# A smaller ring for GpSimd's DMA descriptors, and the last wait moved from GpSimd to SyncE

## The chip, the core and the metric

The kernel runs on one core of one Trainium2 chip. The metric is the time of one execution on the device in microseconds (us), the median of several runs. A core has five engines that run side by side, each with an instruction queue of its own: TensorE (PE, its weight loads as PEld), VectorE (DVE), ScalarE (ACT), GpSimd (POOL) and SyncE (SP). They are ordered among each other by semaphores alone. DMAs are issued by SP, ACT and POOL; those of POOL (here all gathers, scatters and accumulating writes) are prepared by software on GpSimd, which writes their descriptors to a scratch area in on-chip memory (SBUF).

## What is computed

The reference is one layer of a gated vision-language block on 8 sequences of 256 tokens of width 256, cut here to its core:

```python
x = x + jnp.tanh(g_xattn[0]) * _L0_xattn_ref(_layernorm(x), ctx_1024, w_q, w_kv, w_out, b_out)
x = x + jnp.tanh(g_ffn[0]) * _L0_ffn_ref(_layernorm(x), W1, W2, Wr)

# _L0_xattn_ref: 16 heads of 64, keys and values from 120 context rows
attn = softmax(einsum('bnhd,bmhd->bhnm', q, k) * 64 ** -0.5)
out = einsum('bhnm,bmhd->bnhd', attn, v).reshape(b, n, 1024) @ w_out + b_out

# _L0_ffn_ref: a router chooses 2 of 8 experts for each token
topk_vals, topk_idx = jax.lax.top_k(softmax(x @ Wr.T), 2)
h = silu(einsum('btd,efd->btef', x, W1))
y = einsum('btef,edf->bted', h, W2)
out = einsum('bte,bted->btd', gate, y)
```

## The kernel before

**Tiling.** The 2,048 tokens pass through attention in 8 batches of 256. Each batch's result (x2) is stored to the output tensor, its normalized form to a scratch tensor in DRAM, and four scatters (POOL, L611, 32 in all) write its tokens' places into a table sorted by expert. Matrices are split into a high and a low half in float16, so that a product is three matmuls.

**Expert tiles.** Each token is sent to two experts, which makes 39 tiles of 128 rows, each of one expert. For tile t POOL gathers the rows (xg, L678, `gather`), PE transposes them (max_pair, L1896), multiplies by the expert's first matrix (st_bank, L1642, 48 matmuls) and second (o_bank, L1642, 24 matmuls), DVE scales the result (yt, L1489), and POOL adds it to the rows of the output tensor with an accumulating indirect DMA (out, L689, `add`). Two adds may meet the same row, so each add first waits until the one before it has landed (semaphore `y_added`, 16 counts for each). SP loads the first matrix of each tile's expert (w_tile, 1 MB, L454). Four buffers each hold xg, yt and w_tile.

**Order.** Every engine's order is written out by hand. Tiles 0 to 9 are mixed into the attention of the later batches; tiles 10 to 38 run in a loop on PE, DVE and ACT, and unrolled on POOL and SP. In this last stretch POOL's queue is, for each t, `gather(t + 4)` and then `add(t)`; the last four adds have no gather ahead. Two DMAs on POOL's queue (found, L664) read the finished table.

**The end.** POOL's last instruction before the engines meet is a wait for all 39 adds, SP's a wait for the last stores of x2.
Of the kernel before, what the change touches and what calls it, by code (L numbers as in the profile page):

```python
# [35 lines left out]
TILES = TOPK * T // P + E - 1  # L36
# [131 lines left out]
def build(nc, x, ctxT, wq, wkv, wo, bo, gx, gf, w1, w2, wr, out, xn2_dram, table, w1_dram):  # L168
    ctx = ExitStack()
    with ctx:  # L170
        def sem(name):
            return ctx.enter_context(nc.semaphore(name))
# [198 lines left out]
        y_added = sem("y_added")  # L371
# [26 lines left out]
        def _(sp):  # L398
# [118 lines left out]
                load_tile(B - 1, t)  # L517
            sp.wait_ge(x2_out[0], 16 * B)
            sp.wait_ge(x2_out[1], 16 * (B + 1))

        @block.gpsimd
        def _(pool):
# [158 lines left out]
            def add(t):  # L681
                rows = EARLY_B * N if t < EARLY else T + P
                pool.wait_ge(y_done, t + 1)
                if t in (0, EARLY):
                    for i in range(NT):
                        pool.wait_ge(x2_out[i], 16 * ((B if t else EARLY_B) + i))
                if t:
                    pool.wait_ge(y_added, 16 * t)  # L688
                pool.indirect_dma_start(out=out[0:rows], out_offset=bass.IndirectOffsetOnAxis(row_of[:, t:t + 1], 0),  # L689
                                        in_=yt[t % XG][:], in_offset=None, compute_op=ALU.add).then_inc(y_added, 16)  # L690
# [58 lines left out]
            for t in range(LISTED - 1, TILES):  # L749
                if t + XG < TILES:  # L750
                    gather(t + XG)
                add(t)
            pool.wait_ge(y_added, 16 * TILES)

        @block.scalar
        def _(act):
# [1333 lines left out]
```

## Time and profile before

| what | value |
|---|---|
| median of 3 runs | 564.67 us (564.46 to 567.79) |
| span of the profiled execution, first to last instruction | 560.1 us |
| PE busy | 493.7 us, 88% of the span |
| DVE, ACT, POOL busy | 370.2, 371.3, 363.9 us |
| DMAs of GpSimd's queue (q0) | 10.30 MB, 9.5% of the 16 engines' time |
| DMAs of SyncE's queue (q1) | 81.86 MB, 46.7% |

The span counts from the first instruction to the last. The page gives no whole time for the profiled execution; its span is 4.6 us under the median of the runs, and I take that difference as what lies around the span. "Busy" leaves out sequencer instructions such as branches, semaphores and drains, which only a query by source line shows.

### The profile page before, as it was taken

What the parts mean: (1) busy time and instruction counts of PE and PEld (TensorE: products, weight loads), DVE (VectorE), ACT (ScalarE), POOL (GpSimd) and SP (SyncE); (2) the same over time, 40 slices, a digit from 0 to 9 for tenths busy, and PEclk for the clock granted to TensorE, in tenths of its full rate; (3) what the DMA queues carried; (4) which work ended last, traced back from release to release, by engine and by line L of the source; (5) the groups of instructions that cost most, each with busy time, mean ns of one, the idle gap of its engine ahead of it and who ended that gap; (6) DMA issues with size and microseconds to landing.
All of it is one profiled execution on the core that took longest, in us unless ns stands there. A gap on an engine that the chain in (4) does not pass through costs nothing. (4 is left out here: it accounts for less than half of the span.)

```text
span 560.1 us, 17891 instructions
## 1 busy us (share of the span) xinstructions
PE 493.7 (88%) x6630; PEld 438.3 (78%) x6631; DVE 370.2 (66%) x856; ACT 371.3 (66%) x576; POOL 363.9 (65%) x372
## 2 busy tenths in 40 slices
PE   2869799998999999798788997699999999999990
PEld 2757688887888879687567886689898898988980
DVE  5899999898889899699996664343444444343430
ACT  1838999998999899789546674245455464645530
POOL 5466979798989998788978642533544436344531
PEclk9979889999999999999689998799999999999996
DMA  7922506173553625263438598766787877778421
GB/s 286 392 77 84 175 12 219 48 244 59 175 127 119 178 97 168 33 212 73 130 148 201 153 287 145 208 185 186 214 259 201 259 207 232 229 224 244 112 30 17
DMA packets 34846, 93.13 MB, mean 166 GB/s; under 512 B 4967, under 2 KB 24565, under 8 KB 27490
## 3 DMA queue, kind: packets, MB, share of 16 engines
q1 hardware_dynamic: 25634, 81.86, 46.7%
q0 software_dynamic: 8576, 10.30, 9.5%
q8 instruction: 40, 0.66, 0.6%
q10 hardware_dynamic: 576, 0.14, 0.1%
q14 instruction: 20, 0.16, 0.1%
HBM read 74.17 MB, written 18.12 MB: 165 GB/s over the span
## 5 line engine op out<-in xcount | busy, mean ns | idle before, releaser
L689 POOL DMA_INDIRECT out<-yt,row_of x39 | 65.0, 1667 | 115.3 <-DMA out<-yt,row_of 96.5
L1642 PE MATMUL st_bank<-xsT,w_tile 128*128 128x128 f16 x1872 | 114.4, 221 | 4.3 <-issue 3.3
L1480 DVE SCALAR_TENSOR_TENSOR hT<-hf,h_scale,hT 128x512 f16<-128x512 f32 x78 | 58.6, 754 | 88.1 <-ACT hT L974 88.1
L1642 PEld LDWEIGHTS st_bank<-xsT,w_tile 128*128 128x128 f16 x1872 | 109.2, 99 | 7.0 <-issue 5.4
L1642 PE MATMUL o_bank<-w2s,hT 128*128 x936 | 109.9, 274 | 1.2 <-DVE yt L1489 1.1
L1642 PEld LDWEIGHTS o_bank<-w2s,hT 128*128 128x128 f16 x936 | 90.4, 99 | 12.4 <-issue 1.6
L968 ACT ACTIVATE hf<-st_bank,z_scale 128x512 f32<-128x512 f32 x78 | 52.9, 679 | 47.9 <-PE st_bank L1642 40.4
L592 POOL TENSOR_TENSOR pT<-pT 120x512 f16<-120x512 f32 x64 | 77.3, 1221 | 8.0 <-ACT pT L842 7.7
L974 ACT ACTIVATE hT<-hf,h_scale 128x512 f16<-128x512 f32 x78 | 56.3, 722 | 13.1 <-ACT hf L968 4.5
L637 POOL TENSOR_SCALAR stage<-stage,upw 128x512 f32<-128x512 f32 x32 | 55.9, 1748 | 10.5 <-ACT w_hi L941 10.4
L841 ACT ACTIVATE pT<-st_bank,exp_bias,logit_scale 120x512 f32<-120x512 f32 x64 | 50.0, 781 | 12.1 <-PE st_bank L1858 11.6
L842 ACT ACTIVATE pT<-st_bank,exp_bias,logit_scale 120x512 f16<-120x512 f32 x64 | 50.1, 783 | 0.0
L949 ACT ACTIVATE xsT<-max_pair 128x256 f16<-128x256 f32 x39 | 14.9, 382 | 48.8 <-PE max_pair L1896 44.7
L678 POOL DMA_INDIRECT xg<-xn,row_of x39 | 39.8, 1019 | 11.3 <-issue 8.9
L1778 PE MATMUL j_bank<-wos,oT 128*128 128x256 f16 x384 | 45.4, 272 | 0.3 <-DVE oT L1179 0.3
L1642 PE MATMUL o_bank<-v,pT 120*128 120x65 f16 x768 | 35.1, 197 | 11.7 <-DVE o L1367 9.6
L1642 PEld LDWEIGHTS o_bank<-v,pT 120*128 120x128 f16 x768 | 30.3, 99 | 18.2 <-issue 16.2
L611 POOL DMA_INDIRECT table<-entry,slot x32 | 32.9, 1027 | 14.2 <-DVE entry L1324 7.2
L1642 PE MATMUL j_bank<-xnT,wqs 128*128 128x256 f16 x336 | 41.0, 273 | 0.3 <-DVE oT L1179 0.3
L1778 PEld LDWEIGHTS j_bank<-wos,oT 128*128 128x128 f16 x384 | 36.4, 98 | 4.5 <-DVE oT L1179 0.4
L1344 DVE TENSOR_REDUCE max_pair<-max_pair 128x8 f32<-128x960 f32 x32 | 37.0, 1155 | 0.0
L1489 DVE TENSOR_SCALAR yt<-o_bank,gate_y 128x256 f32<-128x256 f32 x39 | 18.9, 483 | 25.4 <-PE o_bank L1642 25.2
(217 smaller groups left out, 966.5 us busy)
## 6 DMA issues: line engine op xcount, KB each, us to landing
w_tile<-w_split SPq DMA_DIRECT2D x39, 1024.0 KB, 5.2
stage<-in_w SPq DMA_DIRECT2D x16, 1024.0 KB, 5.1
w_split<-w_hi SPq DMA_DIRECT2D x8, 512.0 KB, 2.8
w_split<-stage SPq DMA_DIRECT2D x8, 512.0 KB, 3.9
out<-x SPq DMA_DIRECT2D x17, 128.0 KB, 5.4
xin<-in_x SPq DMA_DIRECT2D x8, 256.0 KB, 4.7
w2s<-in_wkv SPq DMA_DIRECT2D x2, 1024.0 KB, 12.2
xres<-in_x SPq DMA_DIRECT2D x16, 128.0 KB
```

Of the source, the lines that this page charges most:

```text
L592: pool.tensor_tensor(pT[g % 2][:, 1, h, :], pT32[:, h, :], pT[g % 2][:, 0, h, :], ALU.subtract).then_inc(pT_low[h], 1)
L637: chain.link(pool.tensor_scalar(chunk, chunk, upw[q % 2][:, i:i + 1], None, ALU.mult))
L678: pool.indirect_dma_start(out=xg[t % XG][:], out_offset=None, in_=xn2_dram[0:rows], in_offset=bass.IndirectOffsetOnAxis(row_of[:, t:t + 1] ...
L689: pool.indirect_dma_start(out=out[0:rows], out_offset=bass.IndirectOffsetOnAxis(row_of[:, t:t + 1], 0), in_=yt[t % XG][:], in_offset=None, ...
L841: nc.scalar.activation(pT32[:, h, :], st_bank[h][0:M, :], ACT.Exp, bias=exp_bias[0:M], scale=logit_scale[0:M])
L842: nc.scalar.activation(pT[g % 2][:, 0, h, :], st_bank[h][0:M, :], ACT.Exp, bias=exp_bias[0:M], scale=logit_scale[0:M]).then_inc(exp_done[h ...
L968: nc.scalar.activation(hf[par][:, cols], z_bank[a][:], ACT.Silu, scale=z_scale[:, bass.ds(t, 1)]).then_inc(silu_done, 1)
L974: nc.scalar.activation(hT[par][:, 0, 4 * a:4 * a + 4, :], hf[par][:, cols].rearrange("p (c n) -> p c n", c=4), ACT.Copy, scale=h_scale[:, ...
L1344: ins = nc.vector.tensor_reduce(both[:, t].rearrange("p (h c) -> p h c", h=2), max_pair[:, :, 0:HP * M].rearrange("p h (c m) -> p h c m", ...
L1480: nc.vector.scalar_tensor_tensor(out=hT[par][:, 1, 4 * a:4 * a + 4, :], in0=hf[par][:, 512 * a:512 * a + 512].rearrange("p (c n) -> p c n" ...
L1642: ins = pe.matmul(out, lhs[i](a), rhs[i](c), start=(i == 0 and a + c == 0), stop=(i == n - 1 and a == 1))
L1778: ins = pe.matmul(dst[:, 0:D], oT[t][:, a, ic, :], wos[:, c, ic, :], start=(ic + a + c == 0), stop=(ic == IC - 1 and a == 1))
```

## The change

```diff
@@ -517,6 +517,7 @@
                 load_tile(B - 1, t)
             sp.wait_ge(x2_out[0], 16 * B)
             sp.wait_ge(x2_out[1], 16 * (B + 1))
+            sp.wait_ge(y_added, 16 * TILES)
 
         @block.gpsimd
         def _(pool):
@@ -750,7 +751,6 @@
                 if t + XG < TILES:
                     gather(t + XG)
                 add(t)
-            pool.wait_ge(y_added, 16 * TILES)
 
         @block.scalar
         def _(act):
@@ -2076,7 +2076,7 @@
...
-    nc = bacc.Bacc("TRN2", target_bir_lowering=False, num_devices=1)
+    nc = bacc.Bacc("TRN2", target_bir_lowering=False, num_devices=1, dynamic_dma_scratch_size=8192)
```

The end of POOL's queue before, as the built program has it (xg is the buffer of gathered rows, yt the scaled result; x5 stands for five adds in a row, the fifth from last with tile 34):

```order
L678 DMA xg<-xn,row_of 128x256 [waits xs_full]
L689 DMA out<-yt,row_of 2176x256 [waits y_added,y_done]
L678 DMA xg<-xn,row_of 128x256 [waits xs_full]
L689 DMA out<-yt,row_of 2176x256 [waits y_added,y_done] x5
L170 UNCONDITIONAL_BRANCH [waits y_added]
```

and now:

```order
L679 DMA xg<-xn,row_of 128x256 [waits xs_full]
L690 DMA out<-yt,row_of 2176x256 [waits y_added,y_done]
L679 DMA xg<-xn,row_of 128x256 [waits xs_full]
L690 DMA out<-yt,row_of 2176x256 [waits y_added,y_done] x5
L170 UNCONDITIONAL_BRANCH
```

POOL's branch to the end has lost its wait; the lines of POOL's code are one higher. The end of SP's queue, as the difference between the two programs:

```order
 L454 ISA
 L454 DMA w_tile<-w_split 128x4096
-L170 UNCONDITIONAL_BRANCH [waits x2_out1,x2_out0]
+L170 UNCONDITIONAL_BRANCH [waits y_added,x2_out1,x2_out0]
```

SP's branch has gained it, and nothing but the branch and SP's drain stands behind it.

## Rows read from the trace of the kernel before

**Rows 1.** Busy time by stretch: start:end, length, PE, PEld, DVE, ACT, POOL, clock, DMA.
```profile
450.00:500.00 50.00, 48.80 (x653) 45.72 (x651) 21.39 (x36) 26.55 (x44) 24.60 (x18) 1.00 0.77 231
500.00:549.00 49.00, 44.73 (x573) 41.15 (x570) 18.94 (x31) 23.26 (x37) 20.78 (x15) 1.00 0.51 129
...
552.00:556.00 4.00, 0.00 (x0) 0.00 (x0) 0.00 (x0) 0.00 (x0) 0.00 (x0) 0.50 0.00 0
556.00:560.10 4.10, 0.00 (x0) 0.00 (x0) 0.00 (x0) 0.00 (x0) 0.00 (x0) 0.50 0.00 0
```

**Rows 2.** Line L170, the end of the program: ns min/median/max, first and last start us.
```profile
L170 SPq COMPARE_BRANCH  x1: 41/41/41, 519.1 to 519.1; - x1
L170 SPq DRAIN  x1: 7/7/7, 519.3 to 519.3; - x1
L170 ACTq DRAIN  x1: 734/734/734, 541.0 to 541.0; - x1
...
L170 DVEq DRAIN  x1: 524/524/524, 546.3 to 546.3; - x1
L170 POOLq COMPARE_BRANCH  x1: 41/41/41, 551.9 to 551.9; - x1
L170 POOLq DRAIN  x1: 7780/7780/7780, 552.1 to 552.1; - x1
```

**Rows 3.** Line L2079, the start of the program, POOL's drain.
```profile
L2079 POOLq DRAIN  x1: 173/173/173, 0.4 to 0.4; - x1
```

**Rows 4.** Instructions of POOL in order of time: start us, us, [idle before, releaser].
```profile
539.19 1.54 POOL L689 DMA_INDIRECT out<-yt,row_of  x1 [2.99 <-DMA out<-yt,row_of]
543.74 1.54 POOL L689 DMA_INDIRECT out<-yt,row_of  x1 [3.01 <-DVE yt L1489]
548.11 1.54 POOL L689 DMA_INDIRECT out<-yt,row_of  x1 [2.83 <-DMA out<-yt,row_of]
```

**Rows 5.** Groups of the page, POOL's DMAs: busy, mean ns, idle before.
```profile
L689 POOL DMA_INDIRECT out<-yt,row_of x39 | 65.0, 1667 | 115.3 <-DMA out<-yt,row_of 96.5
...
L678 POOL DMA_INDIRECT xg<-xn,row_of x39 | 39.8, 1019 | 11.3 <-issue 8.9
...
L611 POOL DMA_INDIRECT table<-entry,slot x32 | 32.9, 1027 | 14.2 <-DVE entry L1324 7.2
```

**Rows 6.** Instructions that touch the table's read-back (found).
```profile
L664 POOL DMA_INDIRECT found<-table,blk x2: 917/977/1037, 273.4 to 360.4; - x2
```

**Rows 7.** DMA queues, 545 to 561 us (two adds): packets, MB, share.
```profile
q0 software_dynamic: 288, 0.26, 14.5%
```

**Rows 8.** Chain of waits, 476 to 491 us: start us, us, what.
```profile
479.13 0.71 issue
479.84 4.19 DMA out<-yt,row_of
...
484.08 1.18 issue
485.25 4.46 DMA out<-yt,row_of
...
489.76 0.71 issue
```

**Rows 9.** POOL's groups from 381.7 us to the end.
```profile
L689 POOL DMA_INDIRECT out<-yt,row_of x30 | 50.0, 1668 | 83.7 <-DMA out<-yt,row_of 78.3 <-DVE yt L1489 3.0 <-issue 2.4
L678 POOL DMA_INDIRECT xg<-xn,row_of x26 | 26.5, 1021 | 7.9 <-issue 5.5 <-PE max_pair L1896 2.4
```

**Rows 10.** Instructions of POOL, 379 to 389 us, in order of time.
```profile
379.92 1.55 POOL L689 DMA_INDIRECT out<-yt,row_of  x1 [4.09 <-DMA out<-yt,row_of]
381.77 1.44 POOL L678 DMA_INDIRECT xg<-xn,row_of  x1 [0.30 <-issue]
388.36 1.57 POOL L689 DMA_INDIRECT out<-yt,row_of  x1 [5.16 <-DMA out<-yt,row_of]
```

**Rows 11.** The PE row that uses the rows gathered at 381.77.
```profile
387.83 0.44 PE L1896 MATMUL max_pair<-ident,xg 128*128 128x128 f32 x2
```

**Rows 12.** Gathers from 370 us on: issue to landing.
```profile
DMA to landing us min/median/max: 2.7/3.3/4.9
```

**Rows 13.** Adds from 360 us on: issue to landing.
```profile
DMA to landing us min/median/max: 3.6/4.8/7.7
```

## The prediction

> **What bounds the kernel now.** I read the busy time by stretch first. From 450 to 500 us PE works 48.80 of 50 us [rows 1]: the expert loop is bound by PE, a tile (48 + 24 + 2 matmuls) taking 50 / (653 / 74) = 5.7 us. The chain of waits names the DMA of the adds for almost all of this stretch, but that is a chain that runs beside PE: an add lands a median 4.8 us after its issue [rows 13], and with the 0.71 us from landing to next issue [rows 8] makes a cycle of 5.5 us, just under PE's 5.7. The change removes nothing from this stretch.
>
> The same view shows what the change aims at: from 552 us to the end at 560.1 us no engine computes and no DMA moves a byte [rows 1]. The page's list of groups cannot say what fills these 8.1 us, as it leaves sequencer instructions out. The query of the end's line does [rows 2]: POOL's branch, held back by its wait for the last add, executes at 551.9 us, and then POOL's DRAIN takes 7,780 ns, from 552.1 to 559.9 us. ACT's drain takes 734 ns and DVE's 524, behind compute of their own. SP's, with 39 tile loads and all the stores and loads of the kernel on its queue before it, takes 7 ns. POOL's first drain, before it has issued a DMA, takes 173 ns [rows 3]. So a drain is not slow for the DMAs' bytes, nor on POOL as such: it is slow on POOL after POOL's DMAs. There are 39 adds, 39 gathers, 32 scatters and 2 reads of the table [rows 5, 6], 112 in all, so 7,780 / 112 = 69 ns for each, if the drain visits every one. That it does so is my inference from these rows.
>
> **What is around it.** The last add is issued at 548.11 us and POOL is done with it at 549.65 [rows 4]; it lands where the branch is released, at 551.9 [rows 2]. From the drain's end to the end of the span are 560.11 - 559.88 = 0.23 us, in which POOL collects and releases the others. The profiled execution stands for the runs: its span is 4.6 us under their median of 564.67, and I keep these 4.6 us.
>
> The Trainium skill, VectorE: DVE Perf Modes, section "The DRAIN you can't avoid", calls the drains of the preamble and postamble "~12 ns constant" on all five engines. By that rule there would be nothing to gain here. The trace agrees for SP (7 ns [rows 2]) and disagrees for POOL by 7,768 ns, and the measurement decides that the time exists; what is left of the rule is a rival below.
>
> **Part 1: the wait goes from POOL to SP.** POOL's branch no longer waits. It follows the last add's issue at 549.65, and the drain starts 0.2 us later, as in rows 2: 549.85 instead of 552.1, so 2.25 us earlier. Behind the wait on SP there is only SP's branch and its 7 ns drain; no load or store queues behind it, and SP has been idle since 519 us [rows 2]. SP sees the landing at 551.9, its branch and drain take 0.2 us, and POOL needs that signal to release the end. So the span cannot end before 552.1 + 0.23 = 552.35 us, which is 7.76 us under 560.11. With the drain as long as now it would end at 549.85 + 7.78 + 0.23 = 557.86, 2.25 us under.
>
> **Part 2: half the scratch.** If the drain visits DMAs that nobody has retired yet, the scratch bounds their number: what has to be overwritten has to be retired first. Each add puts 288 / 2 / 16 = 9 packets on each DMA engine [rows 7], and 112 x 9 = 1,008 for the whole kernel. No row shows how many the scratch holds. Between the ends "as long as now" (7.78 us) and "as short as at the start" (0.17 us [rows 3]), half a scratch that is full at the end means at most half the 112: 56 x 69 ns = 3.9 us, end 549.85 + 3.9 + 0.23 = 553.98, 6.1 us under.
>
 No run yet shows it.
>
> A drain of up to (552.1 - 549.85) / 0.069 = 32 DMAs would be hidden behind the landing. A ring that frees only a part of its entries at a time fills up once more before the end and leaves fewer than 56; one that frees all 56 at the 57th leaves 56 again. The saving is therefore 6.1 to 7.8 us. I take 7.5, because a retirement late in the program is likely with either number of descriptors and anything under 32 entries is worth the full 7.76.
>
> **Part 3: retiring in line.** What the drain no longer does, POOL must do while issuing. Two rows bound it. Above: 3.9 us at once, 56 at the drain's 69 ns. Below: once in the kernel before the step from landing to issue is 1.18 us where it is 0.71 elsewhere [rows 8], 0.47 us more, at the 92nd of POOL's DMAs; that may be one retirement of this kind, since a ring would need it about there if an add took more descriptors than a gather. I take 0.47 us, because a retirement in line needs one look at an old semaphore and not 56.
> Where does it fall? From 381.7 us on there are 30 adds and 26 gathers [rows 9], so the gather at 381.77 us is the 57th DMA, and the first to overwrite if 56 fit. POOL idles 5.16 us behind it [rows 10], so the add chain does not feel it; PE wants those rows at 387.83 [rows 11], and the landing is at most 381.77 + 4.9 = 386.7 [rows 12], 1.1 us early. 0.47 us is hidden; 3.9 us would cost up to 2.8 us. Later retirements on an add lengthen its cycle, which has 0.2 us to PE's 5.7 and four buffers behind it: hidden, unless it is one of the last adds. There the add at 543.74 was released by DVE and the one at 548.11 by the add before [rows 4]; one retirement of 0.47 us between costs 0.1 to 0.3 us.
>
> **The sum.** Outside the tail nothing; tail -7.5; in line +0.2: -7.3, so 564.67 - 7.3 = 557.4 us, a span of 552.8. The cover of part 1 is the last add's flight; were the drain shorter still, the landing at 551.9 is what is late next. Everything in SBUF moves down by 8192 bytes; I cost that at nothing, since all tiles move together and no engine's instruction changes.
>
> The Trainium skill, Runtime: NRT & Kernel Launch, section "The ~15µs preamble/postamble breakdown", puts about 2 us behind a kernel for resetting the DMA rings. If half the ring halved that, the result would be 1 us lower, an estimate from that page, and inside the range; no row shows the time around the span.
>
> **The rivals.**
> - *The drain's length does not depend on the scratch* (it visits all 112, or a fixed area). For: nothing in the trace varies the scratch. Against: nothing. It starts 2.25 us earlier all the same: 562.4 us. Chance 0.12.
> - *The drain is fixed work that starts once the last DMA has landed.* Then the move hides nothing: 564.6 us. The rule of the constant drain belongs here: nothing moves. Against it stand 173 ns at the start and 7,780 at the end. Chance 0.06.
> - *Retiring costs as much in line and meets PE.* The 57th DMA takes 3.9 us more or waits for the add ahead of it; PE stalls 1 to 2.8 us, or several late adds each lose a part of it. 564.67 - 6.1 or 7.5, + 1 to 2.8: 558.2 to 561.4 us. Chance 0.17.
> - *Slower: every DMA behind the 56th waits until the one before it has landed,* as the ring is always full from there. Then a gather waits for the add ahead of it, and the cycle is 4.8 (landing) + 0.7 + 1.0 (gather) + 0.3 = 6.8 us, 1.1 over PE's 5.7 for each of 26 gathers: +29 us, and -6 at the end: 588 us. It decides from the point where the cycle passes 5.7 us. Against: a full ring frees its oldest entry, which landed long ago. Chance 0.03.
>
> **Numbers.** The forecast has 0.62, with a range of its own of 556.6 to 558.8 us. A measurement here tells 1%, 5.65 us, from no change: faster means 559.0 or less. That is the forecast and about 0.04 of the third rival: 0.66. Within 1%: 0.31. Slower: 0.03. The range has to reach from the forecast over the third rival to the first, which leaves 0.09 out: 556.0 (the floor of 556.9 less 0.9 for scatter of the runs, and the ring's reset) to 562.6 us.
>
> **What would show it.** Right: POOL's drain starts within 0.3 us of 549.9 (or the last add's end) and takes under 3.9 us; SP's branch follows the last landing; the span ends 0.4 us behind it. A gather near the 57th DMA, or the step before an add, is longer by some tenths. Wrong: the drain still takes 7.8 us (first rival), starts behind the landing (second), PE waits for xg near 388 us (third), or gathers start only where adds land (fourth).

## The result and the profile after

The changed kernel took 553.78 us in the median of 5 runs (552.65 to 556.34), against 564.67 us before (564.38 to 567.79, 5 runs): ratio 0.9839, 95% interval 0.9801 to 0.9876. (All ratios and intervals here and below leave out executions over 1.5% above the fastest of their kernel, so they are nearer to 1 than the medians, which are of all.) It is faster, as forecast. The forecast of 557.4 us was 3.6 us too high, and the range (556.0 to 562.6) missed the time.

The profiled execution of after has a span of 553.3 us, 6.8 us less than before. The query of the end's line, which answers to [rows 2], shows what went (columns: instructions, ns min/median/max, first and last start us):

```profile
L170 ACTq DRAIN  x1: 732/732/732, 541.4 to 541.4; - x1
...
L170 DVEq DRAIN  x1: 524/524/524, 546.7 to 546.7; - x1
L170 POOLq DRAIN  x1: 4543/4543/4543, 548.5 to 548.5; - x1
L170 SPq COMPARE_BRANCH  x1: 41/41/41, 552.6 to 552.6; - x1
L170 SPq DRAIN  x1: 7/7/7, 552.8 to 552.8; - x1
```

POOL's drain no longer begins behind the landing of the last add. Its record begins at 548.5 us, even before that add's own record, which ends at 550.26; counted from there it takes 548.50 + 4.54 - 550.26 = 2.78 us where before it took 7.78. SP's branch now shows the landing (552.6), where POOL's did.

The page's instruction groups of POOL, which answer to [rows 5], are as they were:

```profile
L690 POOL DMA_INDIRECT out<-yt,row_of x39 | 64.2, 1645 | 115.6 <-DMA out<-yt,row_of 101.9
...
L679 POOL DMA_INDIRECT xg<-xn,row_of x39 | 39.6, 1015 | 11.3 <-issue 9.2
...
L612 POOL DMA_INDIRECT table<-entry,slot x32 | 32.5, 1014 | 15.1 <-DVE entry L1324 8.0
```

So are the stretches of the loop, which answer to [rows 1] (columns as there); the third line is the empty time at the end, of which 0.7 us is left from 8.1:

```profile
450.00:500.00 50.00, 48.74 (x649) 45.64 (x647) 21.66 (x36) 26.49 (x44) 25.04 (x18) 1.00 0.76 229
500.00:549.00 49.00, 45.14 (x580) 41.55 (x577) 18.98 (x31) 23.64 (x38) 19.75 (x15) 1.00 0.52 131
...
552.60:553.20 0.60, 0.00 (x0) 0.00 (x0) 0.00 (x0) 0.00 (x0) 0.00 (x0) 0.50 0.00 0
```

I call **tail** the time from the end of DVE's last yt (tile 38) to the end of the span, and **loop** the time from tile 13's yt to tile 37's. In after the tail is 553.28 - 547.18 = 6.10 us, before 560.11 - 546.77 = 13.34: 7.24 us less. The loop took 136.86 and 136.76 us. The other 0.4 us, by which after is behind, arose before tile 13 (0.3 us: 406.75 against 406.44) and in the loop (0.1).

The chain of waits of after (start us, us, what) shows the one place where the smaller ring is seen at the end, the step of 1.35 us that is 0.71 elsewhere (its add is the 108th of POOL's DMAs):

```profile
525.41 3.88 DMA out<-yt,row_of
...
529.33 1.35 issue
530.68 3.78 DMA out<-yt,row_of
...
534.50 0.71 issue
535.22 3.84 DMA out<-yt,row_of
...
548.01 0.49 issue
548.50 1.76 POOLq L170
```

### The profile page after: what moved, and what is told of

The parts are those of the page before. It is cut to its first block and busy times, and to the rows that moved or that the text cites. A ratio compares the mean times of both kernels' runs of the same rounds, so it can differ in the third digit from the quotient of the medians.

```text
span 553.3 us, 17890 instructions
## 1 busy us (share of the span) xinstructions
PE 494.4 (89%) x6630; PEld 439.5 (79%) x6631; DVE 370.6 (67%) x856; ACT 371.4 (67%) x576; POOL 362.7 (66%) x372
## 5 line engine op out<-in xcount | busy, mean ns | idle before, releaser
L1778 PE MATMUL j_bank<-wos,oT 128*128 128x256 f16 x384 | 46.6, 277 | 0.3 <-DVE oT L1179 0.3
L1642 PE MATMUL j_bank<-xnT,wqs 128*128 128x256 f16 x336 | 42.2, 278 | 0.0
L1642 PEld LDWEIGHTS j_bank<-xnT,wqs 128*128 128x128 f16 x336 | 32.4, 99 | 4.7 <-issue 0.8
```

Of the source, the lines that this page charges most:

```text
L1642: ins = pe.matmul(out, lhs[i](a), rhs[i](c), start=(i == 0 and a + c == 0), stop=(i == n - 1 and a == 1))
L1778: ins = pe.matmul(dst[:, 0:D], oT[t][:, a, ic, :], wos[:, c, ic, :], start=(ic + a + c == 0), stop=(ic == IC - 1 and a == 1))
```

## The experiments

Theory A: the change is worth its tail, some 7.2 us, to which both edits add, and the rest of the 10.9 us between the two medians is scatter of the executions. Rival: something that the profile's span doesn't show, around the span or in the body, gives 3 us more. The others ask what the drain's length hangs on, and what retiring in line costs.

This table is worked out from the trace of each profiled execution (us). "Behind the add" is the time from the end of the last add's record on POOL to the drain's end; "Landing to end" is the time from the last landing of the last add, which releases the branch that waits for it, to the end of the span.

| kernel | scratch | wait on | drain | behind the add | last yt | tail | landing to end |
|---|---|---|---|---|---|---|---|
| before | 16384 | POOL | 7.78 | | 546.77 | 13.34 | 8.21 |
| after | 8192 | SP | 4.54 | 2.78 | 547.18 | 6.10 | 0.73 |
| e1_ring_only | 8192 | POOL | 1.70 | | 549.08 | 7.45 | 2.13 |
| e2_wait_only | 16384 | SP | 9.55 | 7.79 | 545.82 | 10.83 | 5.81 |
| e3_early_drain | 16384 | POOL | 5.52 | | 553.01 | 11.42 | 5.96 |
| e4_after | 8192 | SP | 4.39 | 2.62 | 542.81 | 6.04 | 0.73 |
| e5_ring12k_pool | 12288 | POOL | 3.66 | | 558.49 | 10.54 | 4.1 |
| e6_ring4k_pool | 4096 | POOL | 1.29 | | 542.27 | 6.78 | 1.7 |
| e7_ring6k_sp | 6144 | SP | 4.91 | 3.15 | 548.92 | 6.23 | 1.3 |
| e8_after_again | 8192 | SP | 4.47 | 2.70 | 551.04 | 5.94 | 0.73 |
| e9_late_drain | 16384 | POOL | 0.46 | | 551.82 | 11.91 | 0.9 |

**Either part alone, and both again.** e1_ring_only is before with the last line of the diff alone:

```diff
-    nc = bacc.Bacc("TRN2", target_bir_lowering=False, num_devices=1)
+    nc = bacc.Bacc("TRN2", target_bir_lowering=False, num_devices=1, dynamic_dma_scratch_size=8192)
```

> The wait stays on POOL, the scratch is 8192. Theory A (the drain and what follows the span both grow with the DMAs that are not yet retired): POOL's drain starts 0.2 us behind the last landing, as before, but takes 0.5 to 2.8 us (at most (552.56 - 550.26 + 0.48) / 0.069 = 40 DMAs, from the drain after the change) instead of 7.78, so the span is 5.0 to 7.3 us shorter than 560.1; the time around the span falls to 2 to 3 us, as with the whole change: in all 8 to 11 us faster, 554 to 557 us. Theory B (the drain is fixed work, the change gained by starting it early; what surrounds the span depends on where the last wait stands): drain 7.8 us, no gain, 564 to 565 us.

Its rows of line L170:

```profile
L170 POOLq COMPARE_BRANCH  x1: 41/41/41, 554.4 to 554.4; - x1
L170 POOLq DRAIN  x1: 1696/1696/1696, 554.6 to 554.6; - x1
```

The drain, behind the landing as before, is 1.70 us instead of 7.78: the scratch alone sets this, and the rival of a drain that visits all 112 whatever the scratch is gone. Median 557.93 us (549.78 to 561.84, 10 runs) against 564.19 (556.99 to 572.52, 31 runs) on the same chip; ratio 0.9914, 0.9842 to 0.9986. The tail is 5.9 us shorter, the medians are 6.3 apart; the expected 554 to 557 us were missed by 0.9.

e2_wait_only is before with the other two lines:

```diff
             sp.wait_ge(x2_out[1], 16 * (B + 1))
+            sp.wait_ge(y_added, 16 * TILES)
...
-            pool.wait_ge(y_added, 16 * TILES)
```

> The scratch keeps its default, the wait stands on SP. Theory A: the drain starts about 3.5 us earlier, beside the last add (after the change it stood at 548.5 where the last landing was 552.56), still retires 112 DMAs from the add's end at 549.65 on, 7.8 us, and ends near 557.5: span 557.8, 2.3 us shorter; the time around the span stays as before, so 562.4 us. Theory B (position, not size): the whole gain of 10.9 us, 553 to 555 us. Theory C (the drain's work begins at the last landing): no gain, 564.5 us.

Its rows of line L170:

```profile
L170 POOLq DRAIN  x1: 9551/9551/9551, 546.9 to 546.9; - x1
L170 SPq COMPARE_BRANCH  x1: 41/41/41, 550.9 to 550.9; - x1
```

From the last add's end (548.62) the drain takes 7.79 us, its old length, now beside the flight of 2.2 us: the tail is 2.5 us shorter. So the drain is not work that starts only at the landing, and the second rival is gone too. 561.65 us (555.08 to 571.35, 10 runs), ratio 0.9969, 0.9913 to 1.0025, which is not told from no change. The parts save 5.89 and 2.51 us of tail, together 8.4; both at once save 7.24, since with the short drain only part of it is there to be hidden.

e4_after is the changed kernel, on that chip:

> The changed kernel again, as a measure for the others on this chip: 553 to 556 us, POOL's drain 4.5 us from about 548.5, some 3 us around the span.

It took 556.63 us (550.93 to 560.68, 10 runs), 7.6 under before's median and 0.6 above the expected range; ratio 0.9936, 0.9874 to 0.9998. Its tail is 6.04 us. e8_after_again is the same, on another chip in 5 rounds:

> The changed kernel against the kernel before, five rounds. Theory A (the change acts in the tail alone, 7.2 us between the two profiles' tails of 13.34 and 6.10; the 10.9 us of the first comparison hold 3.7 us of scatter of the executions): 6.5 to 8 us faster, ratio 0.986 to 0.988. Theory B (the change also shortens the rest by 3 to 4 us, through the lower places in SBUF or fewer live descriptors): 10 to 12 us faster, ratio 0.979 to 0.982.

555.95 us (553.26 to 559.05, 6 runs) against 564.01 (556.71 to 567.87, 11 runs): 8.1 us, ratio 0.9887, 0.982 to 0.9954; tail 5.94. By their medians both repetitions lie by the tail's 7.2 us and not by 10.9. Their intervals, 0.1 to 7.1 and 2.6 to 10.2 us, end below 10.9 too, though like the ratios they lie nearer to no change than the medians do; the first ends just under the tail's 7.2 as well.

**Where the executions differ.** The profiled executions of e4 and e8 are of one program and have spans of 548.9 and 557.0 us, with tails 0.1 us apart. Their chains of waits (start us, us, what) part in the flights of the adds, e4_after:

```profile
356.23 4.01 DMA out<-yt,row_of
...
361.03 3.81 DMA out<-yt,row_of
...
366.10 4.26 DMA out<-yt,row_of
...
371.12 4.27 DMA out<-yt,row_of
```

and the same four adds in e8_after_again:

```profile
358.68 5.89 DMA out<-yt,row_of
...
365.37 5.01 DMA out<-yt,row_of
...
370.42 1.22 issue
371.64 5.62 DMA out<-yt,row_of
...
378.01 6.44 DMA out<-yt,row_of
```

They sum to 16.4 us in one and 23.0 in the other; e8 was already 2.5 us behind where the first of them is issued. Each add waits for the last, and gathers stand behind adds on POOL's queue, so PE waits for its rows in e8 (start us, us, then the instruction, and the idle time before it in brackets):

```profile
390.39 0.69 PE L1896 MATMUL max_pair<-ident,xg 128*128 128x128 f32 x2 [4.43 <-DMA xg<-xn,row_of]
```

Busy time from 385 to 405 us (columns as in [rows 1]), e4_after:

```profile
385.00:405.00 20.00, 19.26 (x263) 17.92 (x261) 7.45 (x13) 10.70 (x18) 9.78 (x8) 1.00 0.76 232
```

and e8_after_again:

```profile
385.00:405.00 20.00, 14.73 (x171) 13.41 (x170) 6.13 (x10) 6.68 (x12) 10.22 (x8) 0.91 0.66 190
```

PE, busy all through the same stretch in e4 at a granted 1.00 (2.4 GHz), stands still for 4.4 us in e8 and goes on at a mean of 0.91, part of it at the lower level of 1.2 GHz. By tile 13 e8 is 410.57 - 402.42 = 8.2 us late, and stays so to the end. In the eleven profiled executions tile 13's yt ends between 401.93 and 418.05 us, while the loop behind it takes 136.76 to 136.94 in all of them. So in the profiled executions the scatter lies ahead of tile 13 and is larger than the change. It is not the ring's doing: with the default scratch the 31 times of before spread over 15.5 us, and e5, whose first longer step comes only at its 72nd DMA, shows such a late wait of PE for xg too, 4.9 us at 397.8 (e3 as well, 4.6 us at 392.4, though its extra drain stands ahead of it). Why the same adds fly 4 us once and 6 another time I did not find.

**What sets the drain's length.** e3_early_drain and e9_late_drain keep the default scratch and the wait on POOL, and drain once more on the way, behind POOL's 45th DMA (ahead of tile 3's add) and ahead of the last five adds:

```diff
                 if b == B - 1:
+                    if t == 3:
+                        pool.drain()
                     add(t)
```

> Default scratch, wait on POOL, as before; one more POOL drain ahead of the fourth add (tile 3), where POOL idles 12.2 us for VectorE. 45 of the 112 DMAs have been issued by then. Theory A (a drain's length is the number of DMAs not yet retired, 69 ns each): the early drain takes about 3.1 us behind the landing of the third add and is hidden, the last drain takes (112 - 45) x 69 ns = 4.7 us, the span is 3.1 us shorter; if what surrounds the span grows with the same number, another part of 4 x 45/112 = 1.6 us: 560.0 to 561.5 us. Theory B (the scratch's size sets the drain, whatever is in it): last drain 7.8 us, 564.5 us.

```diff
                 if t + XG < TILES:
                     gather(t + XG)
+                if t == TILES - 5:
+                    pool.drain()
                 add(t)
```

> Default scratch, wait on POOL, one more POOL drain behind the last gather and ahead of the fifth-last add (tile 34), where no idle time covers it. Theory A (retiring is work that moves): that drain takes about 107/112 x 7.78 = 7.4 us behind the landing of the last gather, the last drain 0.3 to 0.7 us (5 DMAs), the last five adds come some 6 us later and catch up little; tail from VectorE's last result to the end 12 to 13.5 us, about as before. Theory B (only the drain at the end is slow, whatever is left to retire): two drains of 7.8 us, tail 19 us or more.

The drains of e3, by their lines (the extra one is L699):

```profile
L699 POOLq DRAIN  x1: 12488/12488/12488, 339.6 to 339.6; - x1
...
L170 POOLq DRAIN  x1: 5523/5523/5523, 558.7 to 558.7; - x1
```

and of e9 (the extra one is L753), with POOL's DMAs around it in order of time:

```profile
L753 POOLq DRAIN  x1: 9979/9979/9979, 530.3 to 530.3; - x1
...
L170 POOLq DRAIN  x1: 460/460/460, 563.0 to 563.0; - x1
```

```profile
531.90 1.00 POOL L678 DMA_INDIRECT xg<-xn,row_of  x1 [0.30 <-issue]
541.07 1.56 POOL L689 DMA_INDIRECT out<-yt,row_of  x1 [8.16 <-issue]
545.88 1.67 POOL L689 DMA_INDIRECT out<-yt,row_of  x1 [3.25 <-DMA out<-yt,row_of]
```

The last drain is shorter by what has been drained before: 5.52 us for the 67 DMAs since, 0.46 us for 5. So the length is in the DMAs not yet retired, which was the inference of part 2, and nothing in the scratch as such. Less the 173 ns of an empty drain [rows 3] it is 57 ns for each of 5, 80 for each of 67, and 68 for each of 112 if none of those was retired before.

e3's tail is 1.9 us shorter, and its median (562.38 us, 558.49 to 566.92, 10 runs) is 1.8 lower (560.0 to 561.5 were expected); its ratio of 1.0004 (0.9954 to 1.0053) is not told from no change. The extra drain was expected to take 3.1 us behind the landing. POOL's DMAs around it:

```profile
339.97 1.59 POOL L689 DMA_INDIRECT out<-yt,row_of  x1 [0.30 <-issue]
352.89 1.57 POOL L689 DMA_INDIRECT out<-yt,row_of  x1 [11.33 <-issue]
```

It can work from 341.56 us, where the 45th DMA is issued, and 45 DMAs at 80 ns each would be done by 345.3. It ends at 352.09. The 45th, an add, lands 10.2 us after its issue, at 350.2: the drain ends 1.9 us behind that and delays the next add by as much. So it seems to have waited for the DMA in flight, and an extra drain cannot simply be put anywhere. e9's, from the gather's end at 532.90 to 540.3, takes 7.4 us and moves the work ahead of five adds that come one by one; the last add starts 7.4 us behind the last yt, and 1.4 us of the tail are won (11.91; one execution, 566.79 us).

**Retiring in line.** e5_ring12k_pool and e6_ring4k_pool are e1 with other sizes, `dynamic_dma_scratch_size=12288` and `=4096`.

> Scratch of 12288 with the wait on POOL. Theory A (the last drain's length is set by the DMAs that are not yet retired, and a ring frees the old ones only where it is full): a ring of three quarters fills once, about the 87th DMA (8.6 by the 57th of the 8192 ring times 1.5), frees the oldest part and leaves some 77 of 112. Last drain 77/112 x 7.78 = 5.3 us, between 4.7 and 6.5; a later and a smaller number of steps of 0.1 to 0.7 us ahead of adds than the 6 of the 8192 ring. Tail from VectorE's last result to the end: 13.3 - 2.4 = 10.9 us. Theory B (length proportional to the ring's bytes): 5.83 us for 12288, but then 3.9 and not 1.70 for 8192, which the run with 8192 alone has already missed. Theory C (a threshold: any ring under the default gives the short drain): 1.7 us.

> Scratch of 4096 with the wait on POOL. Theory A: the ring is full far more often, some 17 DMAs are left at the end, last drain 0.9 to 1.6 us, at most the 1.70 of the 8192 ring; more than twice the 6 in-line steps of the 8192 ring, in all 3 to 5 us of POOL's time against 2.0, none of them before PE's work (loop from tile 13 to 37 stays 136.8 us). Tail 6.5 to 7.5 us against 7.45 with 8192. Rival (slower): with 28 DMAs in the ring a retirement meets DMAs still in flight, PE waits for gathers, the loop from tile 13 to 37 becomes longer than 138 us.

Single executions: 571.86 us (tile 13's yt at 418.05, 12 us behind before's, so the total says nothing of the ring) and 551.98 us. The drains were 3.66 and 1.29 us; for 12288 I had expected 4.7 to 6.5, for 4096 0.9 to 1.6. With 4096 the loop took 136.76 us, as before: the rival there is gone.

What POOL does instead can be read at each add that waits for the one before it. The step from landing to issue is 0.71 us, and longer at these of POOL's DMAs (left out are the 45th and 50th, where POOL's own queue holds the add back in most executions, the 46th of e3 and the 108th of e9, which stand behind the extra drains, and those where DVE's yt came last, as at e9's 53rd):

| scratch | longer steps at DMA number |
|---|---|
| 16384 | 92 (1.18) |
| 12288 | 72, 96, 104, 109 (1.35) |
| 8192 | 53 (1.22), 76, 84, 90, 102, 108 (1.35) |
| 6144 | 66, 74, 80, 88, 94 |
| 4096 | 46, 64, 70, 74, 80, 102 |

I set beside it a ring of scratch / 16 slots in which a gather or scatter takes 9 (the number of [rows 7]), the two reads of the table 2 and 3, and an add 17, a number fitted to the first entries of 16384, 12288 and 8192: the sums pass 1,024, 768 and 512 at just the 92nd, 72nd and 53rd DMA. The Trainium skill, DMA: Bandwidth & Descriptors, section "Terms", gives 16 bytes for a descriptor, and these three entries agree with that. How much the ring frees when it is full no row shows, so the later entries do not test the model, and the number left for the last drain is not known. With the default scratch the model wants 33 DMAs retired from the 92nd on, in one seen step of 0.47 us; the last drain then has 79 and not 112, at 96 ns each. An estimate from 57 to 96 ns is 36 to 61 DMAs for 12288, 16 to 27 for 8192 (e1) and 12 to 19 for 4096. Why the price of one is not the same everywhere is open.

The longer steps of 8192 (0.47, 0.16, 0.14, 0.43, 0.13 and 0.64 us over the step at the same place in before) sum to 2.0 us, where before had 0.47, against 6.1 us of drain that e1 saved. With 4096 I had expected more than twelve steps and 3 to 5 us; seen are six and 1.3 us, though by the estimate above more is retired in line. What retiring costs at the gathers, where the distance from one DMA to the next stays 0.30 us, does not show. In the loop they are covered: with scratches of 4096 to 12288 it takes 136.76 to 136.89 us, as with 16384.

**A smaller ring with the wait on SP.** e7_ring6k_sp is after with `dynamic_dma_scratch_size=6144`:

> The change with a scratch of 6144 in place of 8192: a candidate. Theory A: the ring is full at other places, so the step of 1.35 us in place of 0.71 ahead of the fifth-last add (tile 34), which the 8192 ring has in the tail, can fall earlier; tail 5.8 to 6.1 us against 6.10 and 6.04, ratio to the changed kernel 0.999 to 1.000. Rival: more retirements in line cost PE time, 1 to 3 us slower than the changed kernel.

Its rows of line L170:

```profile
L170 POOLq DRAIN  x1: 4913/4913/4913, 550.0 to 550.0; - x1
L170 SPq COMPARE_BRANCH  x1: 41/41/41, 553.9 to 553.9; - x1
```

Tail 6.23 us where 5.8 to 6.1 were expected, 556.39 us (552.67 to 558.02, 6 runs), ratio 0.9883, 0.9817 to 0.9948, beside e8's 555.95: no better. The drain still ends 1.1 us behind the landing. With 8192 and the wait on SP it ends 0.5 us behind it: the drain's end and not SP's branch is last in all four executions of the two kernels. In after, e4 and e8 the last add lands 2.28, 2.13 and 2.21 us behind the end of its record, and the drain ends 2.78, 2.62 and 2.70 behind it: it moves with the landing, so here too it seems to wait for the last DMA, as e3's extra one did. Why 0.5 us in one place, 1.1 and 1.9 in others come behind the landing is open, and 4096 with the wait on SP was not tried. No version was found that beats the changed kernel.

## Why the direction was right and the size wrong

**The bound and the target: right.** The loop is untouched, and all that the profile lost lies behind the last yt.

**Part 1, the wait to SP: right, with a small miss.** The forecast start of the drain was 549.85 us; the work starts at the last add's end, though its record starts 1.8 us earlier. From landing to the end I had 0.45 us and measured 0.73. My assumption that a short drain would hide fully behind the flight was wrong by this 0.3 us, since its end follows the landing.

**Part 2, the ring: right.** The bound was 3.9 us, the drain 1.70 (e1) or 2.78 beside the flight (after). That a share of the DMAs is left over was right, that each takes nine places was not: the model above needs 17 for an add, with which 52 and not 56 fit into 8192, and 91 and not all 112 into 16384. Of the four rivals the first, a drain of unchanged length, fell with e1, and the second, a drain that starts at the landing, with e2.

**Part 3, in line: right in size, not in place.** Taken were 0.47 us at the 57th DMA, which is a gather; measured was nothing there. POOL's instructions of after from 379 us on, which answer to [rows 10]:

```profile
380.82 1.55 POOL L690 DMA_INDIRECT out<-yt,row_of  x1 [4.00 <-DMA out<-yt,row_of]
382.67 1.01 POOL L679 DMA_INDIRECT xg<-xn,row_of  x1 [0.30 <-issue]
388.19 1.57 POOL L690 DMA_INDIRECT out<-yt,row_of  x1 [4.50 <-DMA out<-yt,row_of]
```

and PE's use of those rows, which answers to [rows 11]:

```profile
388.19 0.38 PE L1896 MATMUL max_pair<-ident,xg 128*128 128x128 f32 x2
```

The steps seen stand at adds, the first at the 53rd, 0.13 to 0.64 us each. The one among the last adds, for which I had 0.1 to 0.3 us, left the last add starting 1.54 us behind the last yt instead of 1.34. The third and fourth rivals (PE stalled, every DMA waiting for the one before) did not come about in the profiled execution: PE's one long wait for xg (8.9 us, to 359.89; before 4.8, to 359.18) lies ahead of the first such step. In e8 PE did wait for a late gather, and the 53rd DMA's step (1.22 in the chain above) lies on the way to it: there the ring can have cost its 0.5 us in the body. No run separates that from the scatter.

**The sum of the tail: -7.5 + 0.2 = -7.3 forecast, -7.24 measured.**

**The step that failed** is the last one, from the profile to the runs: "The profiled execution stands for the runs", with 4.6 us around the span, and the low end "less 0.9 for scatter of the runs". Each later run comes with its own span, and its time is 1.7 to 3.2 us above it, in before (564.28 with 561.2; 556.71 with 554.8) as in after (556.34 with 553.3; 552.65 with 550.6). The median run of after, 553.78 us, has a span of 551.0: of the 3.6 us that the forecast was too high, 1.8 are the span (552.8 forecast) and 1.8 the time around it (4.6 against 2.8). By those 1.7 to 3.2 us the profiled execution of before took about 562 to 563 us, 1.4 to 2.9 less than the median I set it equal to. Its own time is not on record, and none of the five times of that comparison is below 564.38: if it is one of them, it had over 4 us around its span, which no later run shows. And 0.9 us was far too small: executions of before lie between 556.71 and 572.52 us, of after between 550.93 and 560.68, in the profiles by the stretch ahead of tile 13. The five executions behind the 553.78 have spans of 550.6 to 553.3; by the tail of 6.0 their last yt ended at about 545 to 547 us, 2 to 3 us earlier than in the medians of e4 and e8. That the remaining 10.9 - 7.24 = 3.7 us are this scatter is the reading that the two repetitions support; no profile of a median execution of before in the first comparison is there to show it directly. The interval of the first ratio (0.9801 to 0.9876, 7.0 to 11.2 us) holds the tail's 7.24 at its edge.

The Trainium skill, Runtime: NRT & Kernel Launch, section "The ~15µs preamble/postamble breakdown", puts about 2 us behind a kernel for resetting the DMA rings. That half a ring would save 1 us of it, as I had estimated, has no support here: the time around the span is 1.9 to 3.2 us with 16384 and 1.7 to 3.1 with 8192.

## What to carry to other kernels

Ask for the sequencer's instructions at the end of the program: an interval without compute or DMA there can be GpSimd's drain, whose length grows with the software DMAs not yet retired; a smaller descriptor ring moves that work to where GpSimd idles, and a last wait given to an idle engine lets the rest run beside the last flight. An extra drain on the way did not do the same here: it retires all at once, and e3's ended only behind the landing of the DMA in flight. Where a change is worth 1% and executions of one program scatter by 2%, forecast the difference from the part of the trace that repeats (here the tail: 6.10, 6.04 and 5.94 us) and give the range the scatter of the runs, not of the profile.

## What the runs showed of the hardware

- GpSimd's drain took 0.17 us with no DMA behind it, 0.46 with 5, 5.52 with 67 and 7.78 with at most 112; SP's took 7 ns with all its transfers behind it.
- With half the scratch the drain was 6.1 us shorter, and the steps before adds were longer by 2.0 us in sum. Why retiring looks cheaper in line is open.
- The record of GpSimd's drain starts up to 2.0 us before the instruction ahead of it ends (548.50 against 550.26 in after, 339.60 against 341.56 in e3): its duration holds time in which it only stands behind another.
- The same four accumulating DMAs of two executions of one program took 16.4 and 23.0 us from issue to landing in sum; behind the longer ones PE waited 4.4 us for a gather, its granted clock was 0.91 in those 20 us, and tile 13 ended 8.2 us later.
- A drain that ran beside the flight of a DMA ended behind its landing: 0.5 us in three executions with 8192, 1.1 with 6144, 1.9 in e3.
